# A four-layer attention chain: joint values product, output in quadrants, new engine orders, and unread matmuls where TensorE waits

## What is computed

```python
# layer 0: attention of x over [ctx, x], 16 heads; rms norm; MLP 256 -> 1024 -> 256
kv = (concat([ctx, x]) @ kv_w + kv_b);  a = softmax(mask(q @ k / 16)) @ v
a = a @ out_w + out_b + x;  x = gelu(rmsnorm(a) @ w1 + b1) @ w2 + b2 + x
# layer 1: RWKV-like block, 32 heads of 8
xa = ln(x);  sx = previous(xa) - xa                        # along the sequence
xxx = tanh((xa + sx * maa_x) @ maa_w1)                      # five groups of 32
xm_j = xa + sx * (stack_j + xxx_j @ maa_w2_j)               # j = 0..4: the "mixes"
w = exp(-exp(td + tanh(xw @ td_w1) @ td_w2))                # the "decay"
r, k, v, g = xr @ Wr.T, xk @ Wk.T, xv @ Wv.T, silu(xg @ Wg.T)
out_t = r_t (u k_t v_t + s);  s = k_t v_t + w_t s           # scan over the 64 tokens
x1 = x + (groupnorm(out) * g) @ Wo.T
x = x1 + sigmoid(xr2 @ Wfr.T) * (relu(xk2 @ Wfk.T)**2 @ Wfv.T)
# layer 2: single-head attention of x over ctx
p = softmax(x @ wq.T @ (ctx @ wk.T).T / 16)
x = x + alpha * (p @ (ctx @ wv.T)) @ wo.T
# layer 3: grouped attention over ctx, 32 query heads of 8, 8 key heads; layer norm
k, v = ctx @ Wk + bk, ctx @ Wv + bv
x = layernorm(softmax(q k / sqrt(8) + mask) @ v @ Wo + bo + x) * gamma + beta
```

## Time and profile before

| | before |
|---|---|
| median of 3 runs | 1574.29 us (1573.39 to 1576.73) |
| the profiled execution: its own time | 1566.94 us |
| the profiled execution: span | 1565.1 us |
| TensorE busy | 1407.5 us (90%) |
| VectorE busy | 1063.2 us (68%) |
| ScalarE, GpSimd busy | 622.6 us, 618.7 us (40% each) |
| mean granted clock of TensorE | 0.957 of 2.4 GHz |
| moved by DMA | 70.40 MB, of which the weights are one load of 5 MB |

### The profile page before, as it was taken

How to read it: one execution, slowest core, us unless ns; L and a number is a source line. 1 busy time by engine, 2 the same in 40 slices (tenths; PEclk the granted TensorE clock), 3 DMA queues, 4 the chain that set the end, 5 groups by cost and what they waited for, 6 DMA issues and landing times.

```text
span 1565.1 us, 34489 instructions
## 1 busy us (share of the span) xinstructions
PE 1407.5 (90%) x14312; PEld 1084.5 (69%) x14312; DVE 1063.2 (68%) x2073; ACT 622.6 (40%) x1351; POOL 618.7 (40%) x604
## 2 busy tenths in 40 slices
PE   6789989999999999999999999999999999998664
PEld 5567676777777776777777677777767777776443
DVE  2355585867768686776868677785857768686735
ACT  2334433435334443533444353444435335443221
POOL 1052625336161533617163361716336162635210
PEclk9899999999999999999999999999989999999776
DMA  8040403214040321404131140413114041403000
GB/s 298 11 59 14 57 27 52 42 25 73 18 59 26 53 41 25 74 18 59 32 55 33 25 72 18 59 32 56 32 24 73 18 55 35 58 6 58 11 8 7
DMA packets 65787, 70.40 MB, mean 45 GB/s; under 512 B 19808, under 2 KB 54752, under 8 KB 65248
## 3 DMA queue, kind: packets, MB, share of 16 engines
q1 hardware_dynamic: 65632, 68.19, 23.7%
HBM read 30.42 MB, written 4.19 MB: 22 GB/s over the span
## 4 chain that ended last, share of the span: by engine, by line
PE 78%; DVE 10%; ACT 6%; issue 3%; POOL 2%; DMA 1%; POOLq 0%; SPq 0%; DVEq 0%; ACTq 0%
PE pw L454 18%; PE pw L432 14%; PE pw L640 7%; PE pw L634 7%; PE pw L438 4%; PE pw L490 4%; PE pw L576 4%; PE pw L585 4%; PE pw L538 3%; PE pw L443 2%; ACT ptA L857 2%; PE pw L755 2%; DVE ab L1293 2%; DVE big L1272 2%; ACT ptC L859 1%
## 5 line engine op out<-in xcount | busy, mean ns | idle before, releaser
L1293 DVE TENSOR_TENSOR_SCAN ab<-pw,ab 128x256 f32<-128x256 f32 x256 | 159.1, 672 | 73.6 <-ACT ab L967 48.4
L1046 POOL TENSOR_TENSOR ab<-big,kvrg 128x504 f32<-128x504 f32 x128 | 161.1, 1259 | 91.1 <-PE pw L454 58.0
L1082 POOL TENSOR_TENSOR ab<-ab,kvrg 128x512 f32<-128x512 f32 x128 | 162.2, 1273 | 4.7 <-DVE ab L1293 4.6
L1031 POOL TENSOR_TENSOR vtmp_A<-mv_A,eps 128x2 f32<-128x2 f32 x16 | 3.1, 194 | 372.2 <-DVE mv_A L1154 372.2
L1069 POOL TENSOR_TENSOR big<-big,xaB 128x512 f32<-128x512 f32 x80 | 92.5, 1174 | 101.6 <-DVE big L1272 101.5
L432 PE MATMUL pw<-big,wb 128*128 128x256 f32 x512 | 130.9, 406 | 0.0
L634 PE MATMUL pw<-tA,wb 128*128 128x256 f32 x512 | 121.1, 391 | 1.5 <-DVE tA L1237 1.5
L1272 DVE SCALAR_TENSOR_TENSOR big<-pw,wa,sxB 128x256 f32<-128x256 f32 x160 | 67.1, 477 | 77.4 <-PE pw L538 77.3
L432 PEld LDWEIGHTS pw<-big,wb 128*128 128x128 f32 x512 | 99.0, 201 | 26.1 <-issue 9.4
L640 PE MATMUL pw<-wb,ptA 128*128 128x256 f32 x512 | 116.7, 382 | 0.0
L634 PEld LDWEIGHTS pw<-tA,wb 128*128 128x128 f32 x512 | 98.2, 195 | 20.9 <-issue 5.4
(11 more groups left out here) (211 smaller groups left out, 3035.6 us busy)
## 6 DMA issues: line engine op xcount, KB each, us to landing
big<-kvrg SPq DMA_DIRECT2D x256, 128.0 KB, 3.9
hT<-in_h SPq DMA_DIRECT2D x16, 512.0 KB, 4.0
...
```

The lines of the kernel that those rows point to most:

```text
L1046: G.tensor_tensor(ab[i % 4][:, :, :, 1:S], vx[i % 3].rearrange("p j (b s) -> p j b s", b=NB)[:, :, :, 0:S - 1], k, ALU.mult).then_inc(kv_p ...
L1082: G.tensor_tensor(ab[i % 4][:, :, :, :], st[i % 2][:, :, :, :], r, ALU.mult).then_inc(pd_ok, 1)
L1293: last = V.tensor_tensor_scan(st[i % 2][:, j, :, :].rearrange("p b s -> p (b s)"), kn(b5)[:, i // 4, :], ab[i % 4][:, j, :, :].rearrange(" ...
```

## The change

1. **Joint values product.** `m_vo` gets 64 more columns with the weights of `v3`. `l2v` then makes the values of layers 2 and 3 in one product of 320 columns, in two ring buffers instead of one, with the two column halves innermost; ScalarE copies both buffers into `uS`, which also lies elsewhere. The stage `v3` is gone; VectorE spreads the values of layer 3 from `uS` in stage `k3`, and signals `v3_ok`.
2. **One turn.** `l2p` turns the whole 128 x 128 block of exponentials at once.
3. **Output in quadrants.** `l2o` uses row group c and column group e of 64 for its four products, and two ring buffers.
4. **Mixes alternating between row groups.** `mixes(js)` runs the two products of a pair in turn.
5. **The decay.** `pw1`'s tanh is one activation of all 128 partitions; `pw2` makes four products of 128 columns on all rows, with `td2` padded by zeros (256 more columns of weights).
6. **New orders.** All strings of `FLOW` are new, for every engine; a steady turn has 80 stages instead of 81.
7. **Unread matmuls.** `warm(k, n)` runs n matmuls of 256 columns into ring buffer k, once it is free, that nothing reads, ahead of the stages that `WARM` names: 141 once and 3 in each of tiles 2 to 13 (ahead of `norm0`), 177 in all.

```diff
+WARM = {
+    ("q0", 0, 0): 11, ("max0", 1, 0): 11, ("exp0", 1, 0): 5, ("exp0", 1, 1): 2,
+    ("value0", 0, TILES - 2): 2, ("out0", 1, TILES - 1): 4, ("norm0", 0, 0): 1, ("norm0", 0, "round"): 3,
+    ("zturn", 0, 0): 9, ("up", 0, TILES - 1): 1, ("up", 3, 1): 1, ("mix2", 1, TILES - 1): 4,
+    ("cv", 0, 0): 5, ("sum", 0, 1): 3, ("sum", 1, 0): 3, ("scan", 5, TILES - 2): 2,
+    ("scan", 5, TILES - 1): 13, ("oturn", 0, 0): 2, ("scan", 6, 0): 2, ("oturn", 1, TILES - 1): 2,
+    ("outg", 0, TILES - 1): 3, ("cturn", 0, TILES - 1): 7, ("l2k", 0, 0): 2, ("x2turn", 0, TILES - 2): 6,
+    ("x2turn", 0, TILES - 1): 4, ("l2p", 0, TILES - 1): 2, ("q3", 0, TILES - 2): 2, ("q3", 0, TILES - 1): 1,
+    ("exp1", 0, TILES - 2): 8, ("exp1", 0, TILES - 1): 6, ("exp1", 1, TILES - 1): 4, ("out1", 0, 0): 6,
+    ("out1", 1, TILES - 2): 4, ("norm3", 0, TILES - 1): 3,
+}
...
+            def warm(k, n):
+                if k >= FIRST_FREE:
+                    pe.wait_ge(*spare(k))
+                for _ in range(n):
+                    mm(bank(k)[:, 0:C], ident, w("q0", 0), start=True, stop=True)
...
-            def mix(j):
-                f = MIX[j]
-                g = group(f % 4)
+            def mixes(js):
                 for m in range(2):
-                    last = mm(kn((b4, b5)[j % 2])[:, m, :], w("m2", f // 4)[g, m * P:(m + 1) * P], thB[g, f // 4, :], start=True, stop=True)
-                last.then_inc(m2_ps, 1)
+                    for j in js:
+                        f = MIX[j]
+                        g = group(f % 4)
+                        last = mm(kn((b4, b5)[j % 2])[:, m, :], w("m2", f // 4)[g, m * P:(m + 1) * P], thB[g, f // 4, :], start=True, stop=True)
+                        if m == 1:
+                            last.then_inc(m2_ps, 1)
...
                 elif name == "pw2":
                     for m in range(2):
-                        last = mm(kn(b5)[:, m, :], w("td2")[0:64, m * P:(m + 1) * P], thB[0:64, 0, :], start=True, stop=True)
+                        for c in range(TT):
+                            last = mm(kn(b5)[:, m, tok(c)], w("td2", c)[:, m * P:(m + 1) * P], thB[:, 0, 0:P], start=True, stop=True)
...
                 elif name == "l2v":
-                    for b in range(NB):
-                        g = slice(64 * (b % 2), 64 * (b % 2) + 64)
+                    for kk in (k, k + 1):
+                        if kk > k and kk >= FIRST_FREE:
+                            pe.wait_ge(*spare(kk))
                         for c in range(2):
-                            last = mm(kn(bank(k))[g, b // 2, :], hT[t % 3][:, c, b, 0:S], m_vo[:, c, :], start=(c == 0), stop=(c == 1))
-                    last.then_inc(full(k)[0], 1)
+                            for h in range(2):
+                                last = mm(bank(kk)[64 * h:64 * h + 64, 0:C + 64], hT[t % 3][:, c, 2 * h + kk % 2, 0:S], m_vo[:, c, :],
+                                          start=(c == 0), stop=(c == 1))
+                        last.then_inc(full(kk)[0], 1)
...
                 elif name == "l2p":
-                    for c in range(TT):
-                        for e in range(2):
-                            g = slice(64 * e, 64 * e + 64)
-                            last = mm(bank(k)[g, c * S:(c + 1) * S], pbd[g, c, :], ident[g, g], start=True, stop=True)
-                    last.then_inc(full(k)[0], 1)
+                    nc.tensor.transpose(bank(k)[:, 0:P], pbd.rearrange("p t n -> p (t n)"), ident).then_inc(full(k)[0], 1)
                 elif name == "l2o":
+                    pe.wait_ge(*spare(k + 1))
                     for c in range(TT):
+                        g = slice(64 * c, 64 * c + 64)
                         for e in range(2):
-                            g = slice(64 * e, 64 * e + 64)
-                            last = mm(kn(bank(k))[g, c, :], ptb[g, c, :], uS[g, c, :], start=True, stop=True)
-                    last.then_inc(full(k)[0], 1)
+                            last = mm(bank(k + c)[64 * e:64 * e + 64, 0:C], ptb[g, e, :], uS[g, e, 0:C], start=True, stop=True)
+                        last.then_inc(full(k + c)[0], 1)
...
-                elif name == "v3":
-                    for b in range(NB):
-                        for c in range(2):
-                            last = mm(bank(k)[64 * (b % 2):64 * (b % 2) + 64, b // 2 * 64:b // 2 * 64 + 64], hT[t % 3][:, c, b, 0:S], w("v3", c),
-                                      start=(c == 0), stop=(c == 1))
-                    last.then_inc(full(k)[0], 1)
...
             def stage(name, i, t):
+                if warm_count(name, i, t):
+                    warm(NEXT[name, i, t], warm_count(name, i, t))
```

More of the change, by code:

```diff
@@ L74 @@
     + [("gnorm", 0), ("gnorm", 1), ("gnorm", 2), ("gnorm", 3), ("gturn", 0), ("outg", 0), ("norm2", 0)],
-    "C": [(n, 0) for n in ("cturn", "fk", "l2k", "fr", "l2v", "fv", "x2turn", "l2s", "l2p", "l2o", "k3", "v3", "x3turn", "q3")]
+    "C": [(n, 0) for n in ("cturn", "fk", "l2k", "fr", "l2v", "fv", "x2turn", "l2s", "l2p", "l2o", "k3", "x3turn", "q3")]
     + attention(1) + [("norm3", 0)],
@@ L122 @@
 STEADY = 11
-USES = {"q0": 1, "k0": 2, "v0": 2, "out0": 1, "zturn": 2, "up": 1, "down": 1, "cturn": 2, "fk": 1, "l2k": 1, "fr": 1, "l2v": 1, "fv": 1,
-        "x2turn": 1, "l2s": 1, "l2p": 1, "l2o": 1, "k3": 1, "v3": 1, "x3turn": 1, "q3": 1, "out1": 1}
+USES = {"q0": 1, "k0": 2, "v0": 2, "out0": 1, "zturn": 2, "up": 1, "down": 1, "cturn": 2, "fk": 1, "l2k": 1, "fr": 1, "l2v": 2, "fv": 1,
+        "x2turn": 1, "l2s": 1, "l2p": 1, "l2o": 2, "k3": 1, "x3turn": 1, "q3": 1, "out1": 1}
 RING = 2
@@ L155, with upcoming, warm_count @@
 SLOT, TURN = numbers()
+def upcoming():
+    out, k = {}, 0
+    for name, i, t in sequence("PE"):
+        k = SLOT.get((name, i, t), k)
+        out[name, i, t] = k
+        if (name, i, t) in SLOT:
+            k += USES[name]
+    return out
+NEXT = upcoming()
+WARM = {
[9 more added lines that the diff above has]
+}
+def warm_count(name, i, t):
+    return WARM.get((name, i, t if t in (0, 1, TILES - 2, TILES - 1) else "round"), 0)
 def run(engine, stage, order):
@@ L397, in stage @@
                     load_x(t + 2, xB[t % 2], ld_x4[t % 2])
-                elif name == "v3" and t + 3 < TILES:
-                    sp.wait_ge(*full(SLOT["v3", 0, t]))
+                elif name == "k3" and t + 3 < TILES:
+                    sp.wait_ge(*full(SLOT["k3", 0, t]))
                     load_context(t + 3)
@@ L764, in part_c @@
                         pe.wait_ge(*read(SLOT["l2o", 0, t]))
+                        pe.wait_ge(*read(SLOT["l2o", 0, t] + 1))
                     for c in range(2):
@@ L823, in part_c @@
                     pe.wait_ge(e_sb, 4 * TURN[1, t] + 3 + i)
-                    pe.wait_ge(*read(SLOT["v3", 0, t]))
+                    if i == 0:
+                        pe.wait_ge(v3_ok, t + 1)
                     values(1, i)
@@ L942, in part_b @@
                     act.wait_ge(pk_ps, t * 6 + 3)
-                    for c in range(TT):
-                        last = A(thB[0:64, 0, c * P:(c + 1) * P], b5[64 * c:64 * c + 64, 0:P], ACT.Tanh)
-                    last.then_inc(pk_sb, 1)
+                    A(thB[:, 0, 0:P], b5[:, 0:P], ACT.Tanh).then_inc(pk_sb, 1)
                 elif name == "pr":
@@ L993, in part_c @@
                 elif name == "l2v":
-                    A(flat(uS), bank(k)[:, :], ACT.Copy).then_inc(read(k)[0], 2)
+                    for kk in (k, k + 1):
+                        if kk > k:
+                            act.wait_ge(*full(kk))
+                        A(uS[:, kk % 2, :], bank(kk)[:, 0:C + 64], ACT.Copy).then_inc(read(kk)[0], 2)
                 elif name in ("x2turn", "x3turn"):
@@ L1090, in stage @@
                     pool.wait_ge(*read(SLOT[name, i, t]))
+                    pool.wait_ge(*read(SLOT[name, i, t] + 1))
                     G.tensor_tensor(c2[:, :, :], c1[:, :, :], row("bo", TT), ALU.add).then_inc(res_c2, 1)
@@ L1360, in part_c @@
                     for c in range(TT):
-                        last = V.scalar_tensor_tensor(c1[:, c, :], kn(bank(k))[:, c, :], rstd["C"][:, c:c + 1], c2[:, c, :], ALU.mult, ALU.add)
-                    last.then_inc(read(k)[0], 2)
-                elif name == "v3":
-                    k = SLOT[name, i, t]
-                    dve.wait_ge(*full(k))
+                        if c:
+                            dve.wait_ge(*full(k + 1))
+                        V.scalar_tensor_tensor(c1[:, c, :], bank(k + c)[:, 0:C], rstd["C"][:, c:c + 1], c2[:, c, :], ALU.mult, ALU.add).then_inc(read(k + c)[0], 2)
+                elif name == "k3":
+                    dve.wait_ge(*read(SLOT["l2v", i, t]))
+                    dve.wait_ge(*read(SLOT["l2v", i, t] + 1))
                     for e in range(2):
```

90 lines of the change are left out of this document (46 added, 44 removed).

## The result

The changed kernel takes 1561.62 us (median of 5 runs, 1555.09 to 1566.06) against 1574.29 (1573.39 to 1576.73): ratio 0.9914, interval 0.9886 to 0.9942. That is faster by 12.7 us: inside the range of 1522 to 1568, but far from the 28 us of the forecast.

What follows compares the result with a forecast made beforehand. TensorE, busy 90% of the span, was taken as the bound. Arithmetic -11, orders +1, clock in the turns -9, head 0 and tail -9 gave -28 us, from 1574.3 to 1546 us; range 1522 to 1568.

Steps and rivals of the forecast that it cites:

- The clock in the turns: Steady turns: with the mix waits filled, half the loss to the 1.2 GHz level goes, -9 us.
- Arithmetic: Changed matmuls: joint product -4.3, one turn -3.0, quadrants -6.9, alternating mixes 0, decay +3.2; together -11.0 us.
- The quadrants: l2o: all four quadrants run at once, so its steps halve; 0.65 us a turn, saving 6.9 us.
- The orders: Steady turn: waits and unread matmuls 6.0 us against 5.2, less 0.7 for small waits; +0.1 a turn, +1 us.
- The rounds: Three unread matmuls a turn before zturn, 1.4 us: 0.45 cover a wait, 0.95 are on the path.
- The head: Start: losses before q0 and max0's second half set against the half clock of the first 78 us; 0.
- The tail: From 1448.8 us on: full clock would save 19 us, of which unread matmuls win half, -9 us.
- The first: Rival: the clock drops between ruk and out0 instead, zturn's unread work all on the path; 1564 us, chance 0.20.
- The second: Rival: the new order halves the waits, the clock stays, tail -15; 1500 to 1520 us, chance 0.12.
- the third: Rival: slower, as unread matmuls lie on TensorE's path; 1586 us with 40 us uncovered, chance 0.08.
- The fourth: Rival: old mixes run one row group after the other, so alternating saves 20 us more; 1526 us, chance 0.03.
- The fifth: Rival: tail's clock does not return at exp1's transposes, -9 becomes -2; 1553 us, chance 0.52 together with the forecast.

Runs made afterwards that it cites:

- e7: Kernel before plus 44 unread matmuls, two ahead of each of the two mix pairs in tiles 2 to 12; ratio 0.9866 to the kernel before.
- e10: e4 with VectorE's spread of the layer-3 values moved to its stage x3turn, behind scan 7; ratio 1.0281 to the kernel before.
- e11: e10 with the same unread matmuls at the mixes as e7; 1587.84 us, ratio 1.0096 to the kernel before.
- e4: All the new arithmetic in the old orders of every engine, without stage v3 and without unread matmuls; ratio 1.0167 to the kernel before.
- e3: Changed kernel without the three unread matmuls ahead of norm0 in each of tiles 2 to 13; ratio 0.9885 to the kernel before.
- e2: Changed kernel without the 78 unread matmuls of tiles 14 and 15; ratio 0.9981 to the kernel before.
- e1: Changed kernel without any of its 177 unread matmuls; 1571.42 us, ratio 0.9984 to the kernel before.
- e6: e1 with the old tail order (less v3) in every engine, no unread matmuls; ratio 0.9922 to the kernel before.
- e13: e7 with 59 more unread matmuls at the waits of the old tail, tiles 14 and 15; 1541.39 us, ratio 0.9800 to the kernel before.
- e5: e4 with l2p and l2o as before the change (four pieces, two diagonal quadrants, one ring buffer); ratio 1.0333 to the kernel before.
- e9: Changed kernel with the two products of a mix one after the other instead of alternating; ratio 0.9922 to the kernel before.

## Why the forecast's size was wrong

**The clock in the turns.** The cause was right, the size was halved without need. All 11 turns run at 1.00: 1003.6 - 11 x 89.7 = 16.9 us, where half was counted. That the drops hang on the mix waits is shown twice: filling them ends the old kernel's drops from tile 4 on (e7), and takes the 98 us that e10 spends at half clock in the 11 turns down to 14, all of it at `k3` (e11). Whether these waits alone are enough for a drop stays open: e4 has the same two waits (15.2 and 13.6 us) and never drops between 307 and 1184 us, while e10, with the same, drops in each turn.

**Arithmetic.** Forecast -11.0, measured in busy time -17.9: joint product 44.3 to 38.0, turn 7.5 to 5.3, output 19.1 to 10.6, decay 18.0 to 17.1, where I had added 3.2. Some of it is the tail's better clock, but a turn too has 83.3 us of matmuls (e3) against 84.5, 1.2 less where 0.7 was forecast. The quadrants came out as forecast (0.66 us, 0.65 said); here the trace agrees with the Trainium skill ("TensorE: Matmul & The Clock Gate", Part 3) that row and column tiles compose.

**The orders.** Forecast +0.1 us a turn, +1 over 13 turns; this is the first step that failed. Work went from 84.5 to 83.3 us, but idle time from 5.2 to 6.2 (e3), so the new order cost +1.0 us a turn, and the turn went only from 89.7 to 89.5. I traced five of the seven waits, each within 0.2 us, and missed `cturn`'s 0.53 and `k0`'s 0.72 behind `out1`'s buffer, where I took 0.7 off as an estimate for just such waits. The rounds, of which I put 0.95 us on the path, cost no length of a turn. Together the 11 turns came out near the forecast all the same, -17.2 us against -9 + 1 - 11 x 11.0/16 = -15.6. That is luck: the clock gave 8 us more than its term, and the rest, -0.3 instead of -6.6, 6 less.

**The head.** Forecast 0, measured +5.7 at tile 3's `k0` (+3.7 in e2, with the same code up to there). `q0` starts at 12.86 us, as said. Orders and arithmetic had no price of their own in the head's sum: without unread matmuls it is 8.9 us slower than the old one (e1, 245.5), and they give back 3 to 5. e4, with the old order and the new arithmetic, has 245.0, so the order alone isn't to blame; no run separates the two.

**The tail. This is the step that failed most:** "I take half: -9". From tile 14's `k0` to the end the changed kernel's profile has 335.6 us, before 324.9: +10.7. Part of that is this one profile, with its 6.8 us at half clock: e3 has 328.1 us, +3.2, and that isn't -9 either. The unread matmuls did their part (e2 and e1 are 0.7% slower), and from tile 15's `k0` on the clock is at 0.95 where it was 0.87; but I gave the tail's new order no price, and it is about 10 us (e6 against e1): longer waits, and more of the work at half clock if nothing fills them. On the old order the same means give their full amount (e13, 9.6 us by its last stretch against e7's). No run puts them into the old tail behind the new turns.

Head, turns and end add up to -0.8 us, the difference of the two profiled spans. The medians differ by 12.7; where the other 12 us lie, no profile shows.

**The rivals.** The first (the clock drops elsewhere in the turn) is out for the new orders, though its waits between `ruk` and `out0` are there; in the old orders e5 and e11 do drop at such waits. The second was right on the clock, wrong on the waits. Of the third only e3's 0.3% may be a trace, and that is within the noise. The fourth is out: 1.13 us for the first pair, and e9. By the program-order rule of the Trainium skill named there it should have held; the runs disagree. The fifth is out: `exp1`'s transposes take 1.91 us in the tail (1479.76) where they took 3.65; e1, without unread matmuls, waits 3.90 us ahead of them and takes 3.65. So the rule of the Trainium skill on transposes, named with it, is not borne out where unread matmuls stand ahead of them.

**Open:** why e4 keeps its clock and e10 does not; what makes the half clock behind tile 14's `k0` come and go, with the same wait ahead of it; what in the new tail order waits longer, piece by piece.
